# A Swin attention block and a graph convolution block on one core: folded weights, fill products and other banks

## What is computed

```python
xn = layernorm(x over channels);  xw = windows(roll(xn, (-4, -4)))
q, k, v = split(xw @ qkv_w.T + qkv_b)
attn = softmax(q * scale @ k.T + rel_pos_bias + mask)
x = x + unroll(windows_back((attn @ v) @ proj_w.T + proj_b))
y = layernorm(x).reshape(B, C, H, W)          # (tokens x channels) read as an image
y = depthwise3x3(pin_w @ y)                    # 24 -> 126 channels
x = x + pout_w @ (gelu(y[:, :63]) * y[:, 63:])
```

```python
h  = bn(conv1x1(x, w1, b1))
xj = max(0, h - roll(h, s)) over even shifts s along rows, then along columns
h  = gelu(bn(conv1x1(concat([h, xj]), wg, bg)))
h  = bn(conv1x1(h, w2, b2)) + x
out = conv1x1(gelu(conv1x1(h, wf1, bf1)), wf2, bf2)
```

## Time and profile before

| | |
|---|---|
| three timed executions | 270.14, 270.16 and 271.33 us, median 270.16 |
| the profiled execution | 271.48 us device time, span 269.5 us from first to last instruction |
| TensorE | busy 251.5 us (93%), weight loads 156.2 us |
| VectorE | busy 182.8 us (68%) |
| ScalarE | busy 164.0 us (61%) |
| POOL | busy 131.2 us (49%) |
| mean granted TensorE clock | 0.989 of full speed |
| chain that ended last | TensorE 69%, VectorE 19%, DMA 3%, issue 3% |

### The profile page before, as it was taken

How to read it: one execution, slowest core, us unless ns; L and a number is a source line. 1 busy time by engine, 2 the same in 40 slices (tenths; PEclk the granted TensorE clock), 3 DMA queues, 4 the chain that set the end, 5 groups by cost and what they waited for, 6 DMA issues and landing times.

```text
span 269.5 us, 5105 instructions
## 1 busy us (share of the span) xinstructions
PE 251.5 (93%) x1878; PEld 156.2 (58%) x1878; DVE 182.8 (68%) x379; ACT 164.0 (61%) x241; POOL 131.2 (49%) x149
## 2 busy tenths in 40 slices
PE   7859999999999999999999999999999999998971
PEld 7747978789697896978877544334432233211110
DVE  3895677768688686786787564457796436689422
ACT  4878869687796876968614533443444355566861
POOL 8990925117767467751197998202231000208722
PEclk9997999999999999999999999999999999999997
DMA  6901000020020267402675277266012000103312
GB/s 207 242 8 32 0 5 0 2 65 25 21 69 4 54 207 300 146 2 60 217 227 145 58 306 256 54 260 260 7 29 60 0 1 0 29 2 99 97 40 58
DMA packets 11470, 24.64 MB, mean 91 GB/s; under 512 B 6473, under 2 KB 8337, under 8 KB 10582
## 3 DMA queue, kind: packets, MB, share of 16 engines
q1 hardware_dynamic: 9006, 21.91, 25.1%
q0 software_dynamic: 1280, 1.97, 3.1%
q10 hardware_dynamic: 1160, 0.44, 0.7%
HBM read 18.41 MB, written 3.15 MB: 80 GB/s over the span
## 4 chain that ended last, share of the span: by engine, by line
PE 69%; DVE 19%; issue 3%; DMA 3%; ACT 2%; POOL 1%; SPq 1%; POOLq 0%; DVEq 0%; ACTq 0%
PE psum L637 12%; PE psum L646 10%; PE psum L760 9%; PE psum L761 9%; PE psum L666 6%; DVE diff L1155 5%; DVE mx L1153 5%; PE psum L768 3%; PE psum L599 3%; PE psum L799 2%; PE psum L776 2%; PE psum L683 2%; PE psum L823 2%; PE psum L837 2%; PE psum L809 2%
## 5 line engine op out<-in xcount | busy, mean ns | idle before, releaser
L1153 DVE TENSOR_REDUCE mx<-psum 128x6 f32<-128x384 f32 x64 | 35.4, 552 | 26.4 <-PE psum L637 26.3
L637 PE MATMUL psum<-kmv,stq 128*128 128x192 f32 x256 | 48.1, 332 | 0.2 <-issue 0.2
L1268 DVE TENSOR_TENSOR gated<-psum,gel 64x512 f32<-64x512 f32 x32 | 22.1, 693 | 30.9 <-ACT gel L1033 30.6
L637 PEld LDWEIGHTS psum<-kmv,stq 128*128 128x128 f32 x256 | 42.0, 195 | 0.3 <-ACT stq L941 0.3
L1033 ACT ACTIVATE gel<-psum 64x512 f32<-64x512 f32 x32 | 18.9, 591 | 35.5 <-PE psum L761 33.3
L487 POOL TENSOR_TENSOR rstd<-var,power 128x16 f32<-128x16 f32 x7 | 20.5, 2925 | 36.5 <-DVE var L1135 36.0
L1155 DVE TENSOR_TENSOR diff<-psum,mx 128x384 f32<-128x384 f32 x64 | 35.7, 558 | 2.2
L975 ACT ACTIVATE pt<-psum 128x768 f32<-128x768 f32 x32 | 25.9, 811 | 18.3 <-PE psum L646 18.0
L760 PE MATMUL psum<-sta,pk 108*128 108x512 f32 x64 | 34.0, 612 | 0.0
L666 PEld LDWEIGHTS psum<-val,pt 128*64 128x64 f32 x768 | 25.0, 137 | 13.9 <-issue 12.2
L646 PE MATMUL psum<-pk,diff 128*128 128x128 f32 x192 | 28.6, 286 | 4.5 <-DVE diff L1155 3.8
(11 more groups left out here) (121 smaller groups left out, 393.6 us busy)
## 6 DMA issues: line engine op xcount, KB each, us to landing
sta<-scratch SPq DMA_DIRECT2D x12, 576.0 KB
stb<-scratch SPq DMA_DIRECT2D x12, 576.0 KB
xtok<-xt SPq DMA_DIRECT2D x8, 192.0 KB, 3.4
xin<-xw SPq DMA_DIRECT2D x8, 192.0 KB, 5.6
out<-yo POOLq DMA_DIRECT2D x28, 48.0 KB, 1.9
x<-x1s SPq DMA_DIRECT2D x24, 48.0 KB
pk<-pack SPq DMA_DIRECT2D x1, 714.5 KB, 7.5
scratch<-ytok SPq DMA_DIRECT2D x3, 192.0 KB, 2.2
```

Source lines behind the costliest of these rows:

```text
L637: l = mm(s[:, NH * WT * p:NH * WT * (p + 1)], stq[:, m % 2, p, 2 * pair + w, :], kmv[:, m % 2, p, 2 * pair + w].rearrange("k h n -> k (h n ...
L1153: v.tensor_reduce(mx[:, slot, w, :], groups, AX.X, ALU.max).then_inc(max_ready, 1)
L1268: v.tensor_tensor(gated[64 * (b % 2):64 * (b % 2) + 64, c * CH:(c + 1) * CH], bank(conv_bank(u))[64:128], gel[:, u % 4, :], ALU.mult).then ...
```

## The change

There are five edits.

1. Opening. The second half's keys for p = 1 are taken by ScalarE after `exps(0)` (semaphore `last_first_keys`) and no longer by VectorE. `add_up(0, 2)` on VectorE comes after `subtract_max(1)`. `turn_xhat(1)` goes to bank 5 and waits for `val_ready` and not for `first_keys`.
2. Fill products. `idle` takes a bank and a block to multiply; there are 1 (was 2) ahead of `scores(0, 0)`, 6 new ones after it and 3 new ones after `turn_xhat(1)`.
3. Folded weights. The product with `concat([h, h - near])` becomes one with `h` and `near`: the weights of `h` become `wgh + wgx` and those of `near` become `-wgx`. Three VectorE instructions make them after the first chunk. `near` gets four buffers and is what is multiplied and transferred; `xj`, its subtraction and its semaphore go.
4. The last `gated_out` no longer waits for `x2_ready`; `row_minima(5)` comes after `second_residual(7)`.
5. The last `mlp_in` writes banks 2 to 5 and waits for the first half of the GELU before it and for `yo_ready`; `mlp_out` of chunk 6 writes bank 0; the last products write banks 1 and 6.

```diff
-        xj = sb(graph, "xj", [128, 4, CH])
-        near = sb(graph, "near", [128, 2, 8, W])
+        near = sb(graph, "near", [128, 4, 8, W])
...
+        LAST_IN = 2
+
+        def last_out(q):
+            return (1, 6)[q]
...
-            return (4, 2, 3, 3)[c] if c < 4 else 3
+            return (4, 2, 3, 3)[c] if c < 4 else 3 if c < NCH - 2 else 0
...
+                    wait(pe, last_first_keys, pair // 2)
...
-            def idle(count):
+            def idle(count, at, block):
 
                 for _ in range(count):
-                    mm(bank(2, 128), zeros, zeros, start=True, stop=True)
+                    mm(bank(at, 128), block, block, start=True, stop=True)
...
-            idle(16)
+            idle(16, 2, diff[:, 0, 0].rearrange("p w n -> p (w n)"))
             pe.wait_ge(first_in, 16)
             turn_xhat(0)
-            idle(2)
+            idle(2, 2, wt("eye"))
             first_qk()
             make_v(0, 5)
-            idle(2)
+            idle(1, 2, wt("eye"))
             scores(0, 0)
+            idle(6, 2, wt("eye"))
 
             pe.wait_ge(first_queries, 2)
             turn(0)
             scores(0, 1)
-            pe.wait_ge(first_keys, 2)
-            turn_xhat(1, 4)
+            pe.wait_ge(val_ready, 1)
+            turn_xhat(1, 5)
+            idle(3, 6, wt("eye"))
             make_q(1)
...
                 pe.wait_ge(gated_ready, gates_before_out(n))
-                wait(pe, x2_ready, n)
+                if n < NCH - 1:
+                    wait(pe, x2_ready, n)
...
             def grapher_in_rest(c):
-                pe.wait_ge(xj_ready, c + 1)
+                pe.wait_ge(near_ready, 2 * (c + 1))
...
-                wait(pe, gf_ready, 2 * c)
+                wait(pe, gf_ready, 2 * c if c < NCH - 1 else 2 * c - 1)
+                if c == NCH - 1:
+                    pe.wait_ge(yo_ready, c - 1)
                 for b in range(B):
                     rows = slice(32 * b, 32 * b + 32)
-                    l = mm(bank(4 + b)[0:F4], wt("wf1")[rows], x_of(c)[rows], start=True, stop=True)
+                    l = mm(bank((4 if c < NCH - 1 else LAST_IN) + b)[0:F4], wt("wf1")[rows], x_of(c)[rows], start=True, stop=True)
...
             exps(0)
-            take_xs(1, 4)
+
+            act.wait_ge(first_k_made, 2)
+            for h in range(NH):
+                dst, src, own = keys_of(1, h, 0, FIRST_K[1], 4, 8)
+                l = a(dst, src, ACT.Copy, scale=own)
+            l.then_inc(last_first_keys, 1)
+            take_xs(1, 5)
...
-                for p in range(2):
+                for p in range(2 - half):
...
             take_first_k(1)
+            subtract_max(1)
             add_up(0, 2)
-            subtract_max(1)
...
+            v.tensor_tensor(wt("wgh"), wt("wgh"), wt("wgx"), ALU.add).then_inc(weights_summed, 1)
+            dve.wait_ge(weights_summed, 1)
+            v.scalar_tensor_tensor(wt("wg"), wt("wg"), -1.0, wt("wgh"), ALU.mult, ALU.add)
+            v.tensor_scalar(wt("wgx"), wt("wgx"), -1.0, None, ALU.mult)
             v.tensor_tensor(wca, wca, wt("dwa"), ALU.mult)
...
-                wait(dve, xj_ready, c - 1)
...
-                dve.wait_ge(near_ready, 2 * (c + 1))
-                v.tensor_tensor(xj[:, c % 4, :], chunk(stacked[0], c), near[:, par].rearrange("p r w -> p (r w)"),
-                                ALU.subtract).then_inc(xj_ready, 1)
...
             second_residual(6)
+            second_residual(7)
             row_minima(5)
-            second_residual(7)
...
-        p["wg"][own, cols], p["wg"][other, cols] = wg[0:C], wg[C:]
+        p["wg"][other, cols] = wg[C:]
```

More of the change, by code:

```diff
@@ L165, in build @@
         positions_ready, one_ready = sem("positions_ready"), sem("one_ready")
-        first_k_made, first_q_made, first_keys, first_queries = (
-            sem(n) for n in ("first_k_made", "first_q_made", "first_keys", "first_queries"))
+        first_k_made, first_q_made, first_keys, last_first_keys, first_queries = (
+            sem(n) for n in ("first_k_made", "first_q_made", "first_keys", "last_first_keys", "first_queries"))
         roots_ready, folding, folded = sem("roots_ready"), sem("folding"), sem("folded")
+        weights_summed = sem("weights_summed")
         shift_made, shift_ready = sem("shift_made"), sem("shift_ready")
@@ L196, in build @@
         hcopied, hall_ready = sem("hcopied"), sem("hall_ready")
-        near_ready, xj_ready, wg_made = sem("near_ready"), sem("xj_ready"), sem("wg_made")
+        near_ready, wg_made = sem("near_ready"), sem("wg_made")
         w2_made, x3_ready, wf1_made, wf2_made, yo_ready = (
             sem(n) for n in ("w2_made", "x3_ready", "wf1_made", "wf2_made", "yo_ready"))
-        xj_in = [[sem(f"xj_in{n}{a}") for a in range(2)] for n in range(4)]
+        near_in = [[sem(f"near_in{n}{a}") for a in range(2)] for n in range(4)]
         stored = [sem(f"stored{par}") for par in range(2)]
@@ L290, in build, with near_of @@
         out_rows = out.rearrange("b c h w -> (b c) (h w)")
+        def near_of(c):
+            return near[:, c % 4].rearrange("p r w -> p (r w)")
         def x_of(c):
@@ L336, in result_bank, with place_near @@
         def result_bank(c):
-            return (4, 2, 3, 3)[c] if c < 4 else 3
+            return (4, 2, 3, 3)[c] if c < 4 else 3 if c < NCH - 2 else 0
         def gates_before_out(n):
             return 16 * (n // 4) + 10 + 2 * (n % 4)
-        def place_xj(queue, c, a):
-            queue.wait_ge(xj_ready, c + 1)
+        def place_near(queue, c, a):
+            queue.wait_ge(near_ready, 2 * (c + 1))
             for d in range(2):
                 own, other = 64 * a + 32 * d, 64 * a + 32 * (1 - d)
-                queue.dma_start(chunk(stacked[d], c)[other:other + C], xj[own:own + C, c % 4, :])\
-                    .then_inc(xj_in[c % 4][a], 16)
+                queue.dma_start(chunk(stacked[d], c)[other:other + C], near_of(c)[own:own + C])\
+                    .then_inc(near_in[c % 4][a], 16)
         def place_of(u):
@@ L786, in grapher_in_rest @@
             def grapher_in_rest(c):
-                pe.wait_ge(xj_ready, c + 1)
+                pe.wait_ge(near_ready, 2 * (c + 1))
                 for a in range(2):
-                    l = mm(bank(graph_bank(c) + a), wt("wgx")[own_rows(a)], xj[own_rows(a), c % 4, :], start=False, stop=True)
+                    l = mm(bank(graph_bank(c) + a), wt("wgx")[own_rows(a)], near_of(c)[own_rows(a)], start=False, stop=True)
                 l.then_inc(wg_made, 1)
@@ L845, in mlp_last @@
                     for b in range(B):
-                        l = mm(bank(graph_bank(NCH - 1) + q)[32 * b:32 * b + 32, LAST[q]], wt("wf2"), gf[:, 1, b, LAST[q]],
+                        l = mm(bank(last_out(q))[32 * b:32 * b + 32, LAST[q]], wt("wf2"), gf[:, 1, b, LAST[q]],
                                start=True, stop=True)
@@ L1314, in nearest @@
                     for a in range(2):
-                        dve.wait_ge(xj_in[c % 4][a], 32)
+                        dve.wait_ge(near_in[c % 4][a], 32)
                 if c >= 5:
                     dve.wait_ge(rows_ready, c + 1)
-                wait(dve, xj_ready, c - 1)
                 for q in range(2):
                     wm = wmin[:, 8 * c:8 * c + 8, :].rearrange("p (r q) x -> p q r x", q=2)[:, q]
-                    v.tensor_tensor(near[:, par].rearrange("p (r q) (w x) -> p q r w x", q=2, x=2)[:, q],
+                    v.tensor_tensor(near[:, c % 4].rearrange("p (r q) (w x) -> p q r w x", q=2, x=2)[:, q],
                                     hall[:, q, :].rearrange("p (w x) -> p w x", x=2).unsqueeze(1)
@@ L1352, in finish_last @@
                 dve.wait_ge(stored[1], 16 * B * 3)
-                v.tensor_scalar(yo[:, 1, LAST[q]], bank(graph_bank(NCH - 1) + q)[:, LAST[q]], vec_x(X_BF2), None, ALU.add)\
+                v.tensor_scalar(yo[:, 1, LAST[q]], bank(last_out(q))[:, LAST[q]], vec_x(X_BF2), None, ALU.add)\
                     .then_inc(yo_ready, 1)
```

16 lines of the change are left out of this document (7 added, 9 removed).

## The result

The changed kernel takes 267.82 us (median of six executions, 267.81 to 267.85). The kernel before, run on the same chip, takes 270.31 us (six, 270.12 to 271.33). The ratio is 0.990 with an interval of 0.9882 to 0.9918: 1.0% faster. The forecast was 267.8. The profiled execution took 267.85, its span is 265.9 and its mean clock 0.994; the earlier trace rows come from one of 271.48 with a span of 269.5, so 3.6 us of span are to be found.

A forecast was written before the change was run, and what follows sets the result against it. TensorE's work or order was taken to bound the kernel, with slack in opening and tail. 1.68 - 0.55 + 0.15 + 1.87 + 0.48 = 3.63 us off the profiled 271.48 gave 267.85, stated as 267.8; range 266.4 to 269.1.

The forecast's parts named there:

- part 1, the opening: Opening: turn(2) at 24.80 us, held by exps(1), against 26.48; gain 1.68 us, bounds 1.45 to 1.75.
- part 2, the fold: Attention: three added VectorE weight products make turn(6) and everything after it 0.55 us later, bounds 0 to 0.75.
- part 3, the middle: First transferred product: TensorE's gap before it goes as near replaces xj; gain 0.15 us, bounds 0.1 and 0.2.
- part 4, the tail: Tail: 0.57 us from gated_out(7)'s dropped wait plus 1.3 from earlier near(5); gain 1.87, bounds 1.3 and 2.0.
- part 5, the last block: Last block: mlp_in(7) needs only the first half of gelu_f(6); gain 0.48 us, bounds 0.4 and 0.5.
- 0.0 to 0.3: Opening: gain in us at turn(2) against an execution of the kernel before without the clock fall.
- The copy's price: Opening: each of ScalarE's three added 64x256 key copies taken as 0.40 us, 1.2 us together.
- The clock's part: Opening: the fall to 1.2 GHz from 21.0 to 24.5 us cost transposes and scores 0.71 + 1.03 = 1.7 us.
- Rival A: Opening: the clock falls anyway, gain 0.6 us in place of 1.68, time 268.9 us; chance 0.15.
- fits in the gap: Attention: 0.13 us of the fold's added 0.68 falls in the gap before the next maximum, leaving 0.55.
- Rivals D: Attention: the low clock lasts, over 8 us at 1.2 GHz to pass 271.5 us; chance 0.04.
- E: Opening: ScalarE paces beyond exps(1), copies take 0.48 us or more, 268.2 us at most; inside the likeliest case's 0.60.

The follow-up runs named there:

- Experiment 1: The kernel before with only the extra fill products of the change added: 270.19 us, ratio 0.9988.
- experiments 2 and 3: The changed kernel with its added fill products taken back, run twice for more executions: 268.14 and 268.31 us.
- experiment 4: The changed kernel with the three VectorE weight-folding instructions moved from the attention to behind gate(7) of the convolution: 267.57 us.
- Experiment 8: The changed kernel with the xj subtractions and transfers of xj put back and the weight fold taken out: 268.93 us.
- Experiments 6: The changed kernel with the last gated_out waiting for x2_ready again and row_minima(5) again ahead of second_residual(7): 268.51 us.
- experiment 7: The changed kernel with the last mlp_in back in banks 4 to 7, waiting for both halves of the gelu before it: 268.29 us.
- experiment 10: The changed kernel with all six second-half key copies on VectorE again, ahead of subtract_max(1): 267.55 us.
- 9: The changed kernel with exps(1) and the square of block 2 ahead of the query copies take_q(1) on ScalarE: 268.04 us.
- 11: The changed kernel with exps(1) ahead of the query copies and one of ScalarE's last three block 1 key copies moved to VectorE: 267.47 us.

## Why the prediction was right

The terms of the sum, each against what the traces gave:

| term | predicted | measured |
|---|---|---|
| part 1, the opening | 1.68 | 1.40 (1.38 at turn(2)) |
| part 2, the fold | -0.55 | -0.44 |
| part 3, the middle | 0.15 | 0.24 (0.22 behind the convolution's start) |
| part 4, the tail | 1.87 | 1.93 |
| part 5, the last block | 0.48 | 0.45 |
| sum | 3.63 | 3.58 |

The forecast of 267.8 lies much nearer to 267.82 than its terms do to theirs. The opening was counted 0.28 too high, and the fold, the middle and the tail 0.11, 0.09 and 0.06 too low. That these nearly cancel is luck.

**The two kinds of executions.** The prediction read the faster runs of before as those in which the clock does not fall at 21 us. Experiment 1 and the spans of its before bear it out: 268.2 to 268.4 at 0.992 or more, or 269.6 at 0.988 or 0.989. Without this reading the sum would have been set against 270.16, 1.3 us too low. The Trainium skill, TensorE: Matmul & The Clock Gate, Part 1, says that the gate's check runs freely, so that one kernel can differ from run to run; 5 of 42 executions of one kernel with the fall agree with that.

It also means that most of part 1 is no gain over the usual execution. turn(2) at 25.03 stands against 25.17 in experiment 1, so 0.14, inside the "0.0 to 0.3" of the prediction. Against usual executions the span went from 268.3 to 265.9. The tail and the last block give 1.93 + 0.45 = 2.38 of these 2.4 us; the 0.29 lost up to the convolution and the 0.22 gained behind its start nearly cancel.

**Part 1, mis-sized by 0.28.** It came out below its bounds of 1.45 to 1.75. The copy's price was right (0.40 taken, 1.19 for three measured), so was the holder of turn(2), and all behind take_xs(1) on ScalarE did move with it (0.12 there, 0.11 at exps(1)). Three readings were off. ScalarE was taken to be free at 17.35, where the earlier trace rows give 16.64 + 0.81 = 17.45; the copies began at 17.48 and take_xs(1) at 18.70, not 18.57. turn(2) was set 0.05 behind the end of exps(1); it starts 0.14 behind it (24.08 + 0.81 = 24.89). These two put turn(2) at 25.03 and not at 24.80. And the 26.48 that it was counted from is 26.41 in TensorE's timeline. The clock's part, the larger one, was as said: 1.00 in the windows shown, and the eight scores in 1.47 by the timeline, where before's took 2.53 in the fall. The fills cost nothing, as said. Whether they are needed for the clock is not shown; experiments 2 and 3 had no fall without them. Rival A (the clock falls anyway) was not met in any of the 71 executions of kernels with the new opening or the fills. Had the five falls been spread by chance over all 113 executions, all would lie in the 42 of before about once in 165 times (an estimate from these counts). So the fills or the new opening did change it, and which of them is open.

**Part 2, mis-sized by 0.11.** The three instructions start 0.32, 0.21 and 0.14 us ahead of their followers, 0.67 in all (0.68 predicted). The step that failed is the 0.13 that "fits in the gap": it took the gap from the end of the last weight product, and VectorE starts the maximum before that end, so 0.23 were free. 0.67 - 0.23 = 0.44, as turn(6) shows and as experiment 4 gives back there. The negation took 0.22 where the two-tensor products took 0.28 and 0.29. The Trainium skill, VectorE: DVE Perf Modes, section Mode 2×_2P, says that an fp32 `tensor_scalar` within SBUF makes two results a cycle; the trace agrees in direction, 0.06 us less in length. By experiment 4 the fold at this place costs 0.32 at the convolution and 0.25 to 0.3 at the end; the prediction said that nothing gives it back, and 0.12 of the 0.44 is given back.

**Part 3** came out at 0.22 behind the start of the convolution, just over its bound of 0.2. The wait of 0.15 is gone. Experiment 8, with the subtractions back, loses 0.13 of the 0.22 in this stretch (by the distance from the convolution's start to grapher_in(1), against the change); where the other 0.09 come from was not followed.

**Part 4** held in its first steps. gated_out(7) has no wait and `normed` follows 1.85 earlier (233.89 against 235.74), 0.65 of it in the tail. near(5) was usable at 239.77, where before had it at 243.05; with the 1.20 of the earlier parts taken off that is 2.08 earlier; 0.57 + 0.65 + 0.68 = 1.90 was the step. grapher_in(5) has no wait for a transfer. But the tail had gained only 1.62 at that point, not 1.87. The step that failed is the time at which TensorE comes free for grapher_in_rest(4): the prediction has 240.6, and it started at 239.70, which with those 1.20 added is 240.90. Behind gated_out(7) TensorE's products follow each other without a pause up to there (7.99 us from start to start) and move only with it. The wait of grapher_out(4) for its gelu is the same 0.41 as before. So TensorE arrived after the data, not with it. The next block gave 0.50 more, where a pause ahead of grapher_in(6), which the prediction had not counted and experiment 8 brings back with 0.48, went too. Ahead of grapher_in(7) 0.19 of it are lost again, where the trace shows mlp_out(4) lasting 1.26 us and no longer 1.06: it now starts at 248.45, ahead of the end of gelu_f(4) at 246.49 + 2.11 = 248.60. So the total was right by two errors of opposite sign: 0.25 less at block 5, 0.31 more at the next two. Experiments 6 and 8 separate the two causes: 0.69 for the wait and the minima's order, and for the subtractions 1.35 to 1.4, or 1.1 net of the fold, which costs 0.25 to 0.3.

**Part 5** was taken as 0.48 and is 0.45 in the trace and 0.47 by experiment 7. mlp_in(7) is released by VectorE, as said.

Rivals D and E: the low clock never lasted, and the copies took 0.40, so neither applied. What the prediction did not consider is that moving the keys costs rather than gains. It asked whether ScalarE would pace the opening, and answered that it does, but did not ask what the same opening would be with VectorE doing the copies (experiment 10: 0.27 us better).

## What to carry to other kernels

If the profiled execution lies above the median, look for the stretch that accounts for it before summing anything, and compare spans and clocks of the other executions; here 1.7 us at the 1.2 GHz level explained 1.3 us of span, and a sum against the median would have missed. Price a bundle of edits one by one against the bundle without it: one of these (the keys) cost 0.3 us inside a gain. A gain at one place is kept only as far as the next chain of nearly the same length: three experiments gained 0.4 to 0.7 us at a turn and kept none of it, half, or about six tenths (9, 11 and 4).

## What the runs showed of the hardware

**Time outside the span.** The device time exceeds the span by 1.8 to 2.1 us in all 60 executions of kernels with the fills (the change, experiment 1 and all others but 2 and 3). Without them it is over 2.2 in 6 of the 11 executions of experiments 2 and 3, up to 2.5, and in 8 of the 35 of before in the three groups. That is where the higher medians of experiments 2 and 3 come from. So times over 2.2 come in 14 of 46 executions without the fills and in none of 60 with them. That goes with the fills but does not show why: the trace shows nothing outside the span, and the cause is open. If it is the fills, they save up to 0.5 us in some executions for a reason other than the clock.

**The size of a clock fall.** The traced fall lasted about 3.5 us of the opening. It moved turn(2) by 1.24 us (26.41 against 25.17 in experiment 1) and the end by 1.2 to 1.3 (spans of 269.5 and 269.6 against 268.3), not by the 1.7 that the products in it lost: without the fall turn(2) is held by ScalarE for 0.34 (the bracket in experiment 1).
